# Two attentions in one kernel: the queries' order in a tile, and how the value sums are turned

## The reference, cut to what matters

```python
# sa: softmax attention
q = (xn @ Wq + bq).reshape(B, S, H, dk).transpose(0, 2, 1, 3)   # k the same
scores = jnp.einsum('bhsd,bhtd->bhst', q, k) / jnp.sqrt(dk)
att = jnp.einsum('bhst,bhtd->bhsd', jax.nn.softmax(scores, axis=-1), v)
out = att.reshape(S, B, D, H).sum(axis=-1).reshape(B, S, D)     # x = x + out
# ba: a scan over key blocks of 64, carrying out, m, l
M_ij = scores.max(axis=-1, keepdims=True); m_new = jnp.maximum(m, M_ij)
corr = jnp.exp(m - m_new); exp_scores = jnp.exp(scores - m_new)
l_new = chunk_sum * corr + chunk_sum
out_new = out * corr + jnp.einsum('bhqk,bhkd->bhqd', exp_scores, V_blk)
...
return out / l                                                   # then @ out_w.T + out_b
```

## Time and profile before

| what | value |
|---|---|
| median of 3 runs | 3012.55 us (3006.28 to 3018.29) |
| the profiled execution's own time | 3009.39 us |
| its span | 3007.6 us |
| mean granted clock of TensorE | 0.839 |
| busy: TensorE, VectorE, ScalarE, GpSimd | 78%, 63%, 44%, 17% of the span |
| L2068, all heads: loads, products | 192.3 us, 201.3 us busy |

### The profile page before, as it was taken

How to read it: one execution, slowest core, us unless ns; L and a number is a source line. 1 busy time by engine, 2 the same in 40 slices (tenths; PEclk the granted TensorE clock), 3 DMA queues, 4 the chain that set the end, 5 groups by cost and what they waited for, 6 DMA issues and landing times.

```text
span 3007.6 us, 61281 instructions
## 1 busy us (share of the span) xinstructions
PE 2345.3 (78%) x19700; PEld 1301.3 (43%) x19752; DVE 1890.4 (63%) x3795; ACT 1308.9 (44%) x2628; POOL 507.1 (17%) x941
## 2 busy tenths in 40 slices
PE   4369958788887785499999955489999999999855
PEld 3246634666665432234444433133333333333434
DVE  5857565655554476376666645477777777777281
ACT  4211144333332202156666633166666666666322
POOL 4402320333332002011111101000000000000013
PEclk9655567889998697599999977599999999999676
DMA  2232200000000001411111001411111111111000
GB/s 64 75 100 64 66 22 0 7 0 0 0 0 1 7 0 45 143 31 28 27 27 27 22 3 49 137 28 32 28 30 32 27 32 32 27 32 27 2 16 28
DMA packets 146722, 98.97 MB, mean 33 GB/s; under 512 B 61150, under 2 KB 126055, under 8 KB 146602
## 3 DMA queue, kind: packets, MB, share of 16 engines
q1 hardware_dynamic: 146602, 97.35, 12.1%
HBM read 56.85 MB, written 39.85 MB: 32 GB/s over the span
## 4 chain that ended last, share of the span: by engine, by line
PE 57%; DVE 19%; issue 9%; ACT 6%; SPq 5%; POOL 2%; DMA 2%; DVEq 1%; ACTq 0%; POOLq 0%; PEldq 0%
PE psum L2056 10%; PE psum L2044 9%; PE psum L2033 9%; PE psum L2068 6%; SPq L1970 4%; DVE X L1281 2%; PE psum L645 1%; DVE tt_sp L1687 1%; PE psum L405 1%; DVE dn_arena L925 1%; ACT ba_pt L2132 1%; PE psum L634 1%; PE psum L668 1%; PE psum L1604 1%; DVE tt_tsp L1685 1%
## 5 line engine op out<-in xcount | busy, mean ns | idle before, releaser
L2262 DVE TENSOR_REDUCE ba_blockmax<-psum 128x16 f32<-128x1024 f32 x512 | 608.9, 1221 | 183.1 <-PE psum L2033 182.6
L2132 ACT ACTIVATE ba_pt<-psum 128x512 f32<-128x512 f32 x1024 | 541.5, 603 | 272.7 <-PE psum L2044 272.6
L2264 DVE TENSOR_REDUCE sa_negmax<-psum 128x1 f32<-128x1024 f32 x256 | 304.4, 1221 | 151.3 <-PE psum L2033 150.9
L2044 PE MATMUL psum<-ba_qs,ba_ks 64*128 64x512 bf16 x1024 | 339.5, 383 | 72.0 <-DVEq L59 50.9
L2033 PE MATMUL psum<-ba_ks,ba_qs 64*128 64x512 bf16 x1024 | 347.1, 423 | 38.4 <-DMA ba_ks<-ba_kstk 30.6
L2132 ACT ACTIVATE sa_pt<-psum 128x512 f32<-128x512 f32 x512 | 268.2, 602 | 194.1 <-PE psum L2044 120.4
L2056 PE MATMUL psum<-ba_pt,ba_vh 128*32 128x512 f32 x2048 | 278.4, 616 | 0.2 <-ACT ba_pt L2132 0.2
L2033 PEld LDWEIGHTS psum<-ba_ks,ba_qs 64*128 64x128 bf16 x1024 | 123.6, 146 | 306.5 <-issue 301.5
L2033 PE MATMUL psum<-sa_ks,sa_qs 96*128 96x512 bf16 x512 | 207.7, 411 | 41.1 <-DMA sa_ks<-sa_kstk 30.4
L2044 PE MATMUL psum<-sa_qs,sa_ks 128*128 128x512 bf16 x460 | 174.4, 383 | 10.2 <-DVEq L59 8.2
L2044 PEld LDWEIGHTS psum<-ba_qs,ba_ks 64*128 64x128 bf16 x1024 | 77.1, 93 | 174.4 <-issue 150.2
(11 more groups left out here) (477 smaller groups left out, 4165.3 us busy)
## 6 DMA issues: line engine op xcount, KB each, us to landing
ba_qs<-ba_qstk SPq DMA_DIRECT2D x128, 96.0 KB, 2.1
ba_ks<-ba_kstk SPq DMA_DIRECT2D x128, 96.0 KB, 2.2
sa_qstk<-sa_pq SPq DMA_DIRECT2D x48, 128.0 KB
sa_kstk<-sa_pk SPq DMA_DIRECT2D x48, 128.0 KB
sa_qs<-sa_qstk SPq DMA_DIRECT2D x32, 192.0 KB, 2.6
sa_ks<-sa_kstk SPq DMA_DIRECT2D x32, 192.0 KB, 2.7
ba_qstk<-ba_pq SPq DMA_DIRECT2D x48, 128.0 KB, 2.3
ba_kstk<-ba_pk SPq DMA_DIRECT2D x48, 128.0 KB, 2.3
```

The costliest lines, as they stand in the source:

```text
L2044: nc.tensor.matmul(bank(4 + slot), ks[b][K0:P, x_ * P:(x_ + 1) * P], qs[b][K0:P, h * HALF:(h + 1) * HALF], start=True, stop=True).then_inc ...
L2132: nc.scalar.activation(pt[2 * x_ + h][:, :], bank(4 + slot), ACT.Exp, scale=SCALE).then_inc(pt_in, 1)
L2262: ins = nc.vector.tensor_reduce(blockmax[g][:, r, :], src.rearrange("p (n s) -> p n s", s=BLOCK), AXX, ALU.max, negate=True)
L2264: ins = nc.vector.tensor_reduce(negmax[g][:, r:r + 1], src, AXX, ALU.max, negate=True)
```

## The change

A query tile now holds every fourth query of one half: tile r takes queries 512 (r // 4) + 4p + r % 4. The row scores read `qs` with a step of four. Since the row of maxima must stand in the order of the queries, each of its three copies becomes two, one for each half, and the waits count 96 where they counted 48. Four products turn the value sums: 128 columns of `oT`, with a step of four, against both halves of `sel` at once (34 or 18 columns), into partitions 0 to 127. In sa a partition no longer holds the eight queries that lie in one row of X, so SyncE copies `onorm` to a new tile `moved` in two DMAs for each head, and GpSimd's add waits for these. In ba only the reading order in `project_out` changes.

```diff
--- before.py
+++ after.py
@@ -1894,6 +1894,7 @@
     den = k.sb(f"{tag}_den", [P, NTB], ctx=ctx)
     recip = k.sb(f"{tag}_recip", [P, NTB], ctx=ctx)
     onorm = [k.sb(f"{tag}_onorm{g}", [P, NTB, HD], ctx=ctx) for g in range(3)]
+    moved = [k.sb(f"{tag}_moved{g}", [P, D], ctx=ctx) for g in range(3)] if not blocked else None
     stk = {n: nc.dram_tensor(f"{tag}_{n}stk", (N, KR, S), BF16, kind="Internal").ap() for n in "qk"}
     bank = lambda n: k.psum[:, n, :]
     VB = 7
@@ -1910,6 +1911,7 @@
     oT_in, turned, out_read, vh_in = mk("oT_in"), k.free_sem(f"{tag}_turned"), mk("out_read"), mk("vh_in")
     neg_in, corr_in, dcorr_in, added = k.free_sem(f"{tag}_neg_in"), mk("corr_in"), mk("dcorr_in"), k.free_sem(f"{tag}_added")
     normed, all_done = mk("normed"), mk("all_done")
+    moved_in = many("moved_in", 3)
     layer = k.layers
     if blocked:
         xt = layer_norm(k, tag)
@@ -1984,7 +1986,9 @@
             s.wait_ge(mparts_in, n.of(1, 2))
             k.plain(s)
             for z in range(3):
-                s.dma_start(qs[b][MR + z:MR + z + 1, :], mparts[b][:, z, :]).then_inc(m_in[b], 16)
+                for h in range(2):
+                    s.dma_start(qs[b][MR + z:MR + z + 1, h * HALF:(h + 1) * HALF],
+                                mparts[b][:, z, h * GROUP:(h + 1) * GROUP]).then_inc(m_in[b], 16)
 
         def body(n, c):
             if c is None or c < N - 2:
@@ -1995,11 +1999,22 @@
                 load(n.at(2))
             if c is None or c < N - 1:
                 maxima(n.at(1))
+            if not blocked and c != 0:
+                move(n.at(-1))
+
+        def move(n):
+            b = n.c % 3
+            s.wait_ge(normed, n.of(1, 1))
+            k.plain(s)
+            for h in range(2):
+                s.dma_start(moved[b][h * (P // 2):(h + 1) * (P // 2), :], onorm[b][:, h * GROUP:(h + 1) * GROUP, :]).then_inc(moved_in[b], 16)
 
         load(Head(0, 0))
         load(Head(0, 1))
         maxima(Head(0, 0))
         heads(s, body)
+        if not blocked:
+            move(Head(0, N - 1))
 
     def tensor(t):
         t.wait_ge(ready, 2)
@@ -2030,7 +2045,8 @@
             if h == 0:
                 t.wait_ge(rows_free[slot], n.of(4, r // 2 + 1))
                 k.plain(t)
-            last = nc.tensor.matmul(bank(2 * slot + h), qs[b][0:KP, :].rearrange("p (a r) -> p r a", r=NTB)[:, r, :],
+            mine = qs[b][0:KP, r // GROUP * HALF:(r // GROUP + 1) * HALF].rearrange("p (a m) -> p m a", m=GROUP)[:, r % GROUP, :]
+            last = nc.tensor.matmul(bank(2 * slot + h), mine,
                                     ks[b][0:KP, h * HALF:(h + 1) * HALF], start=True, stop=True)
             if h == 1:
                 last.then_inc(rows_in[slot], 1)
@@ -2062,17 +2078,16 @@
             t.wait_ge(oT_in, n.of(1, 1))
             t.wait_ge(*wait)
             k.plain(t)
-            for r in range(NTB):
-                for h in range(2):
-                    lhsT = oT[n.c % 3][:, :].rearrange("p (a r) -> p r a", r=NTB)[:, r, :]
-                    last = nc.tensor.matmul(k.psum[h * 64:(h + 1) * 64, 4 + slot, r * V1:(r + 1) * V1], lhsT, sel[:, h, :],
-                                            start=True, stop=True, skip_group_check=True)
+            out = bank(4 + slot)[:, 0:NTB * V1].rearrange("p (h m e) -> p m h e", h=2, m=GROUP)
+            for m in range(GROUP):
+                last = nc.tensor.matmul(out[:, m, :, :], oT[n.c % 3][:, :].rearrange("p (a m) -> p m a", m=GROUP)[:, m, :], sel[:, :, :],
+                                        start=True, stop=True, skip_group_check=True)
             last.then_inc(turned, 1)
 
         def body(n, c):
             for x_ in range(NTB):
                 if x_ == 0:
-                    t.wait_ge(m_in[n.c % 3], n.third(48, 49))
+                    t.wait_ge(m_in[n.c % 3], n.third(96, 97))
                 lead = n.at((x_ + LEAD) // NTB)
                 r = (x_ + LEAD) % NTB
                 ahead = c is None or lead.c < N
@@ -2170,7 +2185,7 @@
                 for z in range(2):
                     p.wait_ge(rows_free[z], n.of(4, 5))
             if n.c >= 3:
-                p.wait_ge(m_in[g], n.third(48, 1))
+                p.wait_ge(m_in[g], n.third(96, 1))
             k.plain(p)
             c_.step(nc.gpsimd.tensor_copy(mparts[g][:, 0, :], negmax[g][:, :]))
             c_.step(nc.gpsimd.tensor_tensor(mrest[:, :], negmax[g][:, :], mparts[g][:, 0, :], ALU.subtract))
@@ -2195,10 +2210,10 @@
         def add(n):
             if blocked:
                 return
-            p.wait_ge(normed, n.of(1, 1))
+            p.wait_ge(moved_in[n.c % 3], n.third(32, 32))
             k.plain(p)
             xs = k.X[:, bass.ds(n.of(1), 1), :].rearrange("p n d -> p (n d)")
-            nc.gpsimd.tensor_tensor(xs, xs, onorm[n.c % 3][:, :, :].rearrange("p r e -> p (r e)"), ALU.add).then_inc(added, 1)
+            nc.gpsimd.tensor_tensor(xs, xs, moved[n.c % 3][:, :], ALU.add).then_inc(added, 1)
 
         def body(n, c):
             if c is None or c < N - 1:
@@ -2376,7 +2391,7 @@
                 if b >= 2:
                     for z in range(2):
                         a.wait_ge(outp[z], b - 1)
-                dst = oT[b % 2][:, :].rearrange("d (p r) -> d r p", r=NTB)[:, g * GROUP:(g + 1) * GROUP, :]
+                dst = oT[b % 2][:, g * GT:(g + 1) * GT].rearrange("d (p m) -> d m p", m=GROUP)
                 nc.scalar.copy(dst, k.psum[:, g, :].rearrange("d (m p) -> d m p", m=GROUP)).then_inc(taken[g], 1)
 
     def vector(v):
```

## The result

The changed kernel takes 3129.78 us (median of 4 runs, 3115.86 to 3136.14) where the one before takes 3015.09 on the same chip (4 runs): a ratio of 1.0379, 95% interval 1.0337 to 1.0421. It is slower, as forecast, but by 115 us where the forecast of 3071 us means 56: the time lies above the range of 3028 to 3102.

What follows compares the result with a forecast made beforehand. TensorE bounds the kernel now; after the change, ba's loop through the maxima's DMAs would bind. 3009.4 + 68 (ba) - 12 (sa) + 3 (moved sums) - 1 (project_out) = 3067.4, median 3.2 above: 3071 us, range 3028 to 3102.

Steps and rivals of the forecast that it cites:

- The maxima's copies: ba: six DMAs, 0.64 us apart, make TensorE wait; head 14.46 us against 13.37, +68 us over about 62 heads.
- Rival B: ba: no stall, because issue steps fall to some 0.3 us; 2985 us, or 2890 with a short turning; chance 0.10.
- the step of 0.48: ba: each further maxima copy issues 0.48 us behind the last; +0.5 us a head, 3033 us; chance 0.06.
- C: ba: six copies in a row hinder one another; +0.2 to +0.5 us more a head, 3085 to 3105 us; chance 0.10.
- the rest of the period: ba: 9.31 us from first row-score load to next head's first issue, plus 0.12 us from landing to load.
- slack of 0.64 us: ba, kernel before: the third maxima DMA could land 0.64 us later, 2420.15 instead of 2419.51, without delaying TensorE.
- -0.05 for a faster row load: ba: one faster row load, ahead of step 4, shortens the copies' loop by 0.05 us, 14.51 to 14.46 us.
- The turning: Turning of value sums, each head: eight wide load-and-product pairs take 1.90 us, no less than before; upper end 2.2 us.
- Rival A: Turning shrinks to 0.90 us while the DMA wait stays; sa gains 31 x 1.0 us more, 3038 us; chance 0.14.
- would swallow a gain or a loss of that size: ba: the turning lies off the deciding loop, so 1.09 us of new idle time absorbs its change.
- Row loads and sa: Row-score loads fall from 140 towards 93 ns; sa gains 0.39 us a head with the turning, -12 us over 31 heads.
- The moved sums: sa: two added SyncE copies a head are hidden; only the last head's copy shows, +3 us once.

Runs made afterwards that it cites:

- four copies: Kernel before with the first of its three maxima copies issued as two, nothing else changed: ratio 1.0080, 3031.06 us against 3010.89.
- six copies: Kernel before with each of its three maxima copies issued as two of 8-byte pieces; layout, tiles and turning kept: ratio 1.0465, 3144.48 us against 3006.43.
- filled stall: Changed kernel with step 0's first row score computed three times more ahead of ba's wait on the maxima copies: ratio 1.0286, 3087.17 us.
- the copy in order: Changed kernel with ScalarE's copy writing value sums in the order the turning reads, so products read 128 neighbouring columns: ratio 1.0391, 3124.29 us.

## Why the prediction was wrong, step by step

**The maxima's copies.** The mechanism and the issue step were right: the sixth starts 3.10 us behind the first (3.08 foretold) and lands 1.99 later; a copy of 8-byte pieces holds SyncE 601 ns, one of 16-byte pieces 595. Rival B and the step of 0.48 are out, and C too: the spacing did not grow. The dispatch of about 50 ns that rival B took from the Trainium skill (DMA: Bandwidth & Descriptors, section "Anatomy of one DMA — SWDGE (gpsimd) path") is stated there for DMAs that GpSimd issues. SyncE's issues here took 601 ns.

**The term that was mis-sized is the rest of the period**, 9.31 us from restart (TensorE's first row-score load) to first issue and 0.12 from landing to load. They are 9.63 (2502.82 to 2512.45) and 0.19 (2512.45 + 3.10 + 1.99 = 2517.54, load at 2517.73). So the head is 9.63 + 5.09 + 0.19 = 14.91 and not 14.46: +28 us over 62 heads. The 9.31 was read from ba's second head, which is written out ahead of the loop. There the first key score and the first exponential come 0.18 and 0.59 us behind the load at 1965.05:
```profile
1965.23 0.37 PE L2044 MATMUL psum<-ba_qs,ba_ks 64*128 64x512 bf16 x1
...
1965.64 0.60 ACT L2132 ACTIVATE ba_pt<-psum 128x512 f32<-128x512 f32 x1 [2.07 <-PE psum L2044]
```
In the loop they come 0.28 and 0.77 us behind it (2502.82, 2503.10, 2503.59), and the other 0.14 us of the 0.32 lie further on. One and the same kernel shows the step: with four copies it is 9.13 us from first key score to the next first issue in the written-out second head, and 9.38 in the loop. In the written-out heads the waits are on constants, in the loop on values worked out in registers, and after a stall TensorE's sequencer has no lead to hide them in; that this is the reason is argued from code and trace, not tested. The prediction had the 9.45 us of a head in the loop beside it and took the smaller figure; with 9.45 its head would have been 14.60. Its slack of 0.64 us was too large as well: a fourth copy comes 0.64 us later and cost 0.32. The -0.05 for a faster row load on this loop is not seen, either.

**The term that was missing is the clock.** The prediction took the granted clock of before (1.00 in the head of the earlier trace rows) over into a head with 1.1 us more idle time. So it put the clock's cost at nothing, without giving a reason. The experiments with six copies and with the filled stall show that the clock falls because of the stall: 0.41 us a head, 26 us.

**The turning** was right: 1.94 us (1.90), loads of 329 ns for 128 f32 columns 16 B apart. Rival A is out. That the spacing and not the count costs is shown from the other side by the copy in order: 192 ns, 0.8 us a sa head. The 0.90 us for a turning without spacing was too low: it took 0.107 us for 128 contiguous columns, where the rows have 107 ns for 32 columns and 192 for 128; measured are 1.08. That ba's new idle time "would swallow a gain or a loss of that size" was wrong: with less work in ba's head the clock falls further.

**Row loads and sa.** The loads fell from 140 to 110 ns, not to 93: two thirds of the way, so the 8 B step still costs something. The page SBUF — State Buffer of the Trainium skill (section "Door 1: The DMA port swizzle") has two accesses in a 16-byte line at full speed. The trace does not agree: 110 ns for 93. sa's head still gave 0.6 us and not 0.39 (-18 us for -12).

**The moved sums** are hidden, as said: line 2010's copies hold SyncE 598 ns and land after 1.8 us. project_out's eight copies took 1066 ns each for 1081, -0.1 us in all where -1 was taken.

**The sum again**, on the profiled executions: 3067 + 28 + 26 - 6 = 3115, where the changed kernel's took 3136.14. Of the 21 us left, 10 lie ahead of sa's first copy (1297.7 before, 1307.6 after) and 9 between the two attentions (230.4, 239.8 us). Both stretches differ among the other kernels too: sa's first copy starts between 1292.5 and 1308.8 us, and between the attentions lie 228.2 to 237.4 us. They are taken for scatter; nothing here tests it. The median of the changed kernel's runs is 6 us below its profiled one.

## What to carry to other kernels

Before adding a transfer to a loop, write the loop that passes through it as a sum (restart to first issue, last issue, landing, restart) and read each term inside the loop, not in a head written out before it. If the sum exceeds the bound engine's time, start the chain a step earlier before judging the change: here one constant turned 3.8% slower into 0.8% faster, and two steps with the turning in order into 2.7%. And work taken from an engine that waits is not free: its stall grows, and with it the risk of a lower clock.

## What the runs showed of the hardware

- TensorE's granted clock fell behind its stalls. With a stall of 1.4 us in heads of 15 us it went to 0.50 within 2.2 us behind the stall, in nearly every second head, and such a head was 0.9 us longer; with the turning shortened as well, all heads were slow (0.86 over the stretch). Three more products in the stall brought the stretch back to 0.99 and made the kernel faster.
- With stalls of 0.8 us at most it fell 0.5 to 0.8 us behind the end of the turning instead, 2.0 us of TensorE with products of 9 columns, and less often (4, 9 and 7 heads with three, four and five copies); that cost 0.2 us a head at most. With the turning in order and an earlier lead it fell once in the same heads.
- The price of a column in a weight load of 128 f32 columns was (329 - 79) / 128 = 1.95 ns at 16 B apart and (192 - 79) / 128 = 0.88 in order; by the same working it had been (217 - 79) / 64 = 2.16 at 32 B. By the spacing of the loads in the turning it was (1.94 - 0.329) / 7 / 128 = 1.80 ns for 1.86. So halving the step from 32 to 16 B gained little. For bf16: 93 ns in order, 110 at 8 B, 140 at 16 B.
- Halving the pieces of a 128-piece copy from 16 to 8 bytes changed neither its issue (595, 601 ns) nor its landing (2.0 us).
